# A transformer block on one core: keys and queries stored unsplit and split a group ahead, half of the weight pieces quantised in the first part

## The chip, the cores and the metric

One NeuronCore of a Trainium2 chip runs the whole program. The metric is the device time of one execution in microseconds (us); lower is better. Two changes are told apart only where they differ by more than the spread of repeated runs.

## The reference, cut to what matters

Input x is (8, 1024, 512) fp32. The block is x + attention(layernorm(x)), then x + ffn(layernorm(x)). Attention has 16 heads, a latent of 128 for queries and one for keys and values, 32 plain and 16 rotated dimensions per head, a causal mask and a clip of the scores at +-80. The rotated key part is shared by all heads. The feed-forward part quantises activations and weights to FP4 in blocks of 16.

```python
c_q, c_kv = x @ W_DQ, x @ W_DKV
Qc, Kc, V = heads(c_q @ W_UQ), heads(c_kv @ W_UK), heads(c_kv @ W_UV)
Qr, Kr = rope(heads(c_q @ W_QR)), rope(x @ W_KR)
scores = clip(concat(Qc, Qr) @ concat(Kc, Kr).T, -80, 80)
out = softmax(causal(scores) / sqrt(48)) @ V @ W_O
# feed-forward: every operand goes through
scale = maximum(max(abs(xb)) / 6, 1e-12)          # xb: blocks of 16
q = GRID[searchsorted(MID, abs(xb / scale))] * sign(xb) * scale
```

## The kernel before

Three parts follow each other, with a barrier at each seam. Every large product is made of three passes over operands split into a rounded part (hi) and its rest (lo): hi x hi, hi x lo, lo x hi.

**Projections** (`projections`, lines 119 to 511): 16 blocks of 512 tokens (8 batches, 2 halves), written once and looped. A block is a list of units, `UNITS1` (line 113): C (both latents, 24 matmuls 512 wide), KR (12), X0 and X1 (16 transposes of the normalised rows of the *next* block), K0, K1, Q0, Q1 (6 each), R0, R1 (rotated queries, 6 each) and V0, V1 (6 each): 84 matmuls and 16 transposes. All units go round four two-bank slots of PSUM. TensorE (lines 448 to 511) works through the list; every engine has the list in its own order of code and waits on counters. ScalarE (292 to 336) casts a unit's bank to hi; VectorE (338 to 446) subtracts it to give lo (`c_lo` line 414, `xt_lo` 373, `kq_out` 442), multiplies the rotated parts by the tables (424 to 430), and computes the next block's row statistics (`row_stats`, 343) and normalised rows (`normalise`, 356, in the code right after C). GpSimd (257 to 290) raises the variances to the power -1/2 (266), adds the two rotated products (285) and, after ScalarE's cast (334), subtracts for their lo (288). SyncE (205 to 255) loads x and stores hi and lo of keys and queries (244), of the rotated parts (238, 247), and V (250). `turned` holds the rotated products. C needs the previous block's X units, X needs the normalised rows, K0 needs `c_lo`.

**Attention** (`attention`, 574 to 1004): 32 groups of 4 heads of one batch, in 12 steps each (`STEPS`, 520): query half 0 with 4 key tiles, half 1 with 8; the diagonal steps are 512, 384, 256 and 128 wide. At step k TensorE makes the scores of k + 1 (20 matmuls, 956) and then weighs step k - 1: P V into `ps_o` (971) and the row sums into `ps_d` (985). ScalarE takes the exponentials (772) and copies `ps_o` out (782); three PSUM slots are shared by score pairs, so the scores of step k + 1 wait for the first exponential of step k. VectorE clips (823, 831), adds pairs of steps (841), turns `ps_d` (848), inverts (852), turns back (856) and normalises (863). In its list by step (875 to 930) stand also the eight instructions that quantise one piece of the feed-forward weights (128x528) per group: reduce 884, scale 889, reciprocal 895, ties 899, product 903, then, after ScalarE's multiply (799), mask 917, two rounding steps 921 and 925, product 930. SyncE (667 to 731) loads a group with 15 transfers (4 for keys and queries in hi and lo, 8 for rotated queries, 2 for rotated keys, 1 for V) and a piece, during the group before, and stores pieces and results.

**Feed-forward** (`feed_forward`, from 1027) is not touched by the change. `fp4_scales` (86) and `fp4_round` (97) are the helpers it shares with the change: `fp4_round` is a mask (100) and two rounding steps (102, 104), each behind a wait for the one before (`own`). GpSimd there multiplies by the inverse scales (1209), released by VectorE's line 94.

## Time and profile before

| | us |
|---|---|
| median of 3 runs | 3201.62 (3198.46 to 3202.04) |
| the profiled execution | 3199.42 |
| its span, first to last instruction | 3197.6 |

| busy, of the span | us | share |
|---|---|---|
| TensorE | 3045.5 | 95% |
| TensorE weight loads | 2234.2 | 70% |
| VectorE | 2604.2 | 81% |
| ScalarE | 1221.9 | 38% |
| GpSimd | 668.1 | 21% |

Engines in the rows: PE is TensorE, PEld its weight loads, DVE VectorE, ACT ScalarE, POOL GpSimd, SPq SyncE's queue. A timeline row gives start and length in us, engine, line, instruction, output and inputs, form, how many were merged (xN), and in brackets the idle time before it and what ended it. Matmuls overlap, so their rate is read from starts. A row by line and form ends with busy us, mean ns of one, and the idle time before. In the table by stage each engine has its busy us and its count of instructions; then come the granted clock of TensorE (1.00 is full), the DMA engines' share and GB/s.

### The profile page before, as it was taken

To read this page: it belongs to the slowest core of one execution; us is meant where nothing else is said; L and a number is where in the kernel's file an instruction comes from. 1 tells how busy PE (TensorE), PEld (TensorE's weight loads), DVE (VectorE), ACT (ScalarE), POOL (GpSimd) and SP (SyncE) were. 2 spreads that over 40 slices of the span, in tenths; PEclk is the share of its full clock that TensorE was granted. 3 is DMA by queue.
4 is the path that set the end of the run, shared out by engine and by line. 5 is a ranking of instruction groups with operands and counts; after the bars stand their busy time and mean duration, and the time that the engine had idled before them with its cause. 6 is when DMAs were issued, how large, how long until landed. Compare 5 with 4: busy or idle time off the path is not lost.

```text
span 3197.6 us, 65496 instructions
## 1 busy us (share of the span) xinstructions
PE 3045.5 (95%) x23492; PEld 2234.2 (70%) x23492; DVE 2604.2 (81%) x4427; ACT 1221.9 (38%) x1830; POOL 668.1 (21%) x634
## 2 busy tenths in 40 slices
PE   7999679999999999978999999999999999999999
PEld 6777534444444444446888888888888888888887
DVE  6777457888888888887888888888888888888886
ACT  3444346666666666652222222222222222222221
POOL 2334300000000000012332332232322222223322
PEclk9999889999999999998999999999999999999999
DMA  6999956665656666651000000000000000000000
GB/s 234 334 338 341 314 151 170 161 182 160 184 169 160 179 167 181 172 160 50 30 25 28 30 26 29 30 30 30 30 30 30 30 30 30 30 30 30 30 24 14
DMA packets 234506, 351.37 MB, mean 110 GB/s; under 512 B 17616, under 2 KB 117840, under 8 KB 234448
## 3 DMA queue, kind: packets, MB, share of 16 engines
q1 hardware_dynamic: 234448, 350.59, 35.9%
q8 instruction: 37, 0.61, 0.1%
q14 instruction: 21, 0.17, 0.0%
HBM read 205.55 MB, written 144.97 MB: 110 GB/s over the span
## 4 chain that ended last, share of the span: by engine, by line
PE 54%; DVE 1%; ACT 0%; issue 0%; POOL 0%; DVEq 0%
PE p_ring L1464 30%; PE p_ring L1492 15%; PE p_ring L1444 5%; PE p_ring L1482 2%; PE p_ring L1472 1%; DVE sb_wg_lo L1391 0%; PE p_ring L1504 0%; DVE sb_fp_tmp L102 0%; DVE sb_xq L1351 0%; DVE sb_h_amax L88 0%; DVE sb_stage L1362 0%; DVE sb_ht_lo L1380 0%; DVE sb_xq L1337 0%; DVE sb_stats L1326 0%; DVE sb_xq L104 0%
## 5 line engine op out<-in xcount | busy, mean ns | idle before, releaser
L772 ACT ACTIVATE sb_probs<-scores 128x1024 f32<-128x1024 f32 (+3 forms) x768 | 586.0, 813 | 395.9 <-PE scores L956 384.9
L1464 PE MATMUL p_ring<-sb_wg_hi,sb_xq_hi 128*128 128x512 f32 (+1 forms) x1536 | 458.5, 379 | 0.3 <-DVE sb_wd_lo L1391 0.3
L1464 PE MATMUL p_ring<-sb_wg_lo,sb_xq_hi 128*128 128x512 f32 (+1 forms) x1536 | 448.9, 373 | 0.0
L1464 PE MATMUL p_ring<-sb_wg_hi,sb_xq_lo 128*128 128x512 f32 (+1 forms) x1536 | 447.9, 373 | 0.0
L831 DVE TENSOR_SCALAR sb_probs<-sb_probs 128x2048 f32<-128x2048 f32 (+3 forms) x320 | 288.3, 901 | 91.6 <-ACT sb_probs L772 88.5
L971 PE MATMUL ps_o<-sb_probs,sb_v 128*32 128x512 f32 (+3 forms) x3072 | 328.1, 499 | 0.0
L1209 POOL TENSOR_TENSOR sb_stage<-sb_stage,sb_h_inv 128x512 f32<-128x512 f32 (+1 forms) x192 | 210.6, 1097 | 542.0 <-DVE sb_h_inv L94 542.0
L956 PEld LDWEIGHTS scores<-sb_q_hi,sb_k_hi 32*128 32x128 f32 x1536 | 73.7, 182 | 345.4 <-ACT sb_probs L772 284.4
L1464 PEld LDWEIGHTS p_ring<-sb_wg_hi,sb_xq_lo 128*128 128x128 f32 x1536 | 285.5, 188 | 41.5
L1464 PEld LDWEIGHTS p_ring<-sb_wg_lo,sb_xq_hi 128*128 128x128 f32 x1536 | 285.0, 188 | 41.1
L1464 PEld LDWEIGHTS p_ring<-sb_wg_hi,sb_xq_hi 128*128 128x128 f32 x1536 | 277.0, 189 | 36.3 <-issue 0.7
L1262 ACT ACTIVATE sb_stage<-p_ring 128x512 f32<-128x512 f32 (+1 forms) x192 | 106.7, 556 | 468.3 <-PE p_ring L1464 468.2
L1492 PE MATMUL p_ring<-sb_wd_hi,sb_ht_hi 128*128 128x512 f32 x704 | 280.2, 398 | 2.2 <-DVE sb_ht_lo L1380 2.2
L1492 PE MATMUL p_ring<-sb_wd_hi,sb_ht_lo 128*128 128x512 f32 x704 | 274.5, 390 | 0.0
L1492 PE MATMUL p_ring<-sb_wd_lo,sb_ht_hi 128*128 128x512 f32 x704 | 274.1, 389 | 0.0
L823 DVE SCALAR_TENSOR_TENSOR sb_probs<-sb_probs,sb_bound 128x512 f32<-128x512 f32 x256 | 174.6, 682 | 121.9 <-ACT sb_probs L772 121.9
L956 PE MATMUL scores<-sb_q_hi,sb_k_hi 32*128 32x512 f32 (+3 forms) x1536 | 172.6, 439 | 89.3 <-DMA sb_v<-v 40.1
L1215 POOL TENSOR_TENSOR sb_stage<-sb_stage,sb_h_scale 128x512 f32<-128x512 f32 (+1 forms) x192 | 189.7, 988 | 267.8 <-DVE sb_stage L104 267.8
L1275 ACT CAST sb_ht_hi<-p_ring 128x1024 fp32r<-128x1024 f32 (+1 forms) x128 | 95.1, 744 | 384.0 <-PE p_ring L1482 384.0
L743 POOL TENSOR_TENSOR sb_wo_lo<-sb_x,sb_wo_hi 128x2048 fp32r<-128x2048 f32 x1 | 9.3, 9316 | 1008.0 <-ACT sb_wo_hi L802 1008.0
L102 DVE SCALAR_TENSOR_TENSOR sb_fp_tmp<-sb_stage 128x512 f32<-128x512 f32 (+1 forms) x192 | 206.0, 1073 | 6.6
L1253 ACT ACTIVATE sb_stage<-sb_stage 128x512 f32<-128x512 f32 (+1 forms) x192 | 113.9, 593 | 215.5 <-POOL sb_stage L1209 215.5
(141 smaller groups left out, 5957.4 us busy)
## 6 DMA issues: line engine op xcount, KB each, us to landing
kq<-sb_kq_out SPq DMA_DIRECT2D x64, 1024.0 KB, 8.6
sb_xin<-in_L_attn_x_dram SPq DMA_DIRECT2D x32, 512.0 KB, 5.9
...
```

What stands on the lines that cost most here:

```text
L102: dve.scalar_tensor_tensor(out=tmp, in0=big, scalar=1.5, in1=y, op0=ALU.max, op1=ALU.add).then_inc(sem, 1)
L772: act.activation(probs[:, k % PROBS, 2 * pair:2 * pair + 2, off:BANK], scores[(2 * k + pair) % RING2][:, :, off:BANK], ACT.Exp, scale=SCAL ...
L823: i = dve.scalar_tensor_tensor(out=pr, in0=pr, scalar=P_MIN, in1=bound[:].unsqueeze(1).to_broadcast([P, NI, P]), op0=ALU.max, op1=ALU.min)
L831: i = dve.tensor_scalar(pr, pr, P_MAX, P_MIN, ALU.min, ALU.max)
L956: mm = pe.matmul(scores[(2 * k + i // 2) % RING2][:, i % 2, off:BANK], key[s][rows, keys], query[s][rows, queries], start=(n == 0), stop=( ...
L971: mm = pe.matmul(ps_o[rows, off:BANK], v_sb[s][:, j, rows], probs[:, k % PROBS, i, off:BANK], start=(j == 0), stop=last)
L1209: pool.tensor_tensor(x, x, spread(h_inv[:, a // QB:b // QB], (b - a) // QB), ALU.mult).then_inc(h_y, 1)
L1215: pool.tensor_tensor(x, x, spread(h_scale[:, a // QB:b // QB], (b - a) // QB), ALU.mult).then_inc(h_q, 1)
L1253: act.mul(h_big[:, h_slot(r, s), 0:b - a], h[:, a:b], MAGIC).then_inc(h_magic, 1)
L1444: i = pe.matmul(ps[:, 0, :], at[a][:, g, :], wo[b][:, g, :], start=(g == 0 and a == b == 0), stop=(g == GROUPS - 1 and a == 1))
L1464: i = pe.matmul(ps[:, m, 0:b0 - a0], xt[a][:, c, :], wg[b][:, m, c, a0:b0], start=(c == 0 and a == b == 0), stop=(c == DC - 1 and a == 1))
L1492: i = pe.matmul(ps[:, 0, :], ht[a][:, c, :], wd[b][:, c, :], start=(c == 0 and a == b == 0), stop=(c == FC - 1 and a == 1))
```

## The change

**First part.** Keys and queries are stored once, unsplit: ScalarE copies the bank to fp32 and frees it, and VectorE's subtraction is gone. C becomes C0 (keys' and values' latent) and C1 (queries'), each with its own cast and rest. The even and odd halves of the rotated pairs are now kept in separate planes, so one unit R (6 matmuls) gives both; VectorE multiplies each of its two banks by two table planes at once (two instructions, 1024 wide), and GpSimd's addition and subtraction and ScalarE's cast for R are 1024 wide. The banks are freed through two counters. One weight piece per block is quantised: `fp4_scales` and a product after X1, ScalarE's multiply after Q1, `fp4_round` and a product after R; SyncE loads and stores it behind the block's stores. The rope table has four planes in place of two, the weights one 256-column stretch less.

**Attention.** A group's keys and queries come with two transfers into `kq_raw`, issued two bodies ahead when the buffer's last split is done. ScalarE rounds them at steps 1 and 2 of the group before, VectorE takes the rest at steps 3 and 9, and TensorE waits for both at step 0. The 16 pieces left take two groups each: scales in the even one, rounding in the odd. Half 0 is turned at step 4 (before: 3), inverted and turned back at step 10 (4, 5), normalised at step 11 (6), ahead of the turning of half 1. Pieces are stored from step 4 of odd groups; in the last body W_O and the third part's first loads are issued behind that store.

```diff
-UNITS1 = ["C", "KR", "X0", "X1", "K0", "K1", "Q0", "Q1", "R0", "R1", "V0", "V1"]
+UNITS1 = ["C0", "C1", "KR", "X0", "X1", "K0", "K1", "Q0", "Q1", "R", "V0", "V1"]
 UNITS1_LAST = [u for u in UNITS1 if u[0] != "X"]
-HI1 = ["C", "X0", "X1", "K0", "K1", "Q0", "Q1", "V0", "V1"]
+HI1 = ["C0", "C1", "X0", "X1"]
+FREED_BY_ACT = ["K0", "K1", "Q0", "Q1", "V0", "V1"]
+FREED_BY_DVE = ["C0", "C1", "KR", "X0", "X1", "R"]
...
-            sp.dma_start(cos_sin[:], t["rope"].rearrange("k p t -> p k t")).then_inc(s_rope, 16)
+            sp.dma_start(qr_raw[:], t["W_QR"]).then_inc(s_w, 16)
+            sp.dma_start(rope[:], t["rope"].rearrange("k p t -> p k t")).then_inc(s_rope, 16)
             sp.wait_ge(xin_free, 2)
             load_x(0, 1)
+            sp.dma_start(piece_in[:], t["w_all"][0]).then_inc(piece_loaded, 16)
...
-                    for s in range(2):
-                        sp.dma_start(kq_v[k, s, b, :, :, cols], kq_out[:, half, k, s]).then_inc(stored[half], 16)
-                sp.wait_ge(rope_lo, n * 3 + 3 + 3)
+                    freed(sp, n, name)
+                    sp.dma_start(kq_v[k, b, :, :, cols], kq_out[:, half, k]).then_inc(stored[half], 16)
+                sp.wait_ge(rope_lo, n * 2 + 2 + 2)
                 for s in range(2):
-                    sp.dma_start(rq_v[s, b, :, :, cols], r_out[:, half, s]).then_inc(stored[half], 16)
-                sp.wait_ge(ps_free, unit(n, units.index("V1")) + RING1 + 1)
+                    for c in range(2):
+                        sp.dma_start(rq_v[s, c, b, :, :, cols], r_out[:, half, s, c]).then_inc(stored[half], 16)
+                freed(sp, n, "V1")
                 for j in range(4):
                     sp.dma_start(v_v[b, half * 4 + j],
                                  v_out[:, half, j].rearrange("p (g d) -> p g d", g=GROUPS)).then_inc(stored[half], 16)
+                if not last:
+
+                    sp.wait_ge(piece_ready, n + 1)
+                    sp.dma_start(piece_in[:], t["w_all"][n + 1]).then_inc(piece_loaded, 16)
+                sp.wait_ge(piece_done, n + 1)
+                sp.dma_start(t["wq_all"][n], piece_y[:]).then_inc(piece_stored, 16)
...
+                for k, name in enumerate(("KR", "R")):
                     if name == "KR":
-                        tu = turned[0:DR, k]
-                        lo = kr_out[0:DR, half, 1, :]
-                        hi = kr_out[0:DR, half, 0, :]
+                        a, b_ = turned_kr[:, 0, :], turned_kr[:, 1, :]
+                        hi, lo = kr_out[0:DR, half, 0, :], kr_out[0:DR, half, 1, :]
                     else:
-                        tu = turned[:, k]
-                        lo = r_out[:, half, 1, k - 1, :]
-                        hi = r_out[:, half, 0, k - 1, :]
-
-                    pool.wait_ge(ps_free, unit(n, units.index(name)) + RING1 + 1)
-                    pool.tensor_tensor(tu[:, 0, :], tu[:, 0, :], tu[:, 1, :], ALU.add).then_inc(rope_sum, 1)
-
-                    pool.wait_ge(rope_hi, n * 3 + k + 1)
-                    pool.tensor_tensor(lo, tu[:, 0, :], hi, ALU.subtract).then_inc(rope_lo, 1)
+                        a, b_ = turned[:, 0], turned[:, 1]
+                        hi, lo = r_out[:, half, 0], r_out[:, half, 1]
+
+                    (freed_last if last else freed)(pool, n, name)
+                    pool.tensor_tensor(a, a, b_, ALU.add).then_inc(rope_sum, 1)
+
+                    pool.wait_ge(rope_hi, n * 2 + k + 1)
+                    pool.tensor_tensor(lo, a, hi, ALU.subtract).then_inc(rope_lo, 1)
...
-                        act.copy(kq_out[:, half, k, 0, 2 * m:2 * m + 2, :].bitcast(F32R), ps[:]).then_inc(act_hi, 1)
+                        act.copy(kq_out[:, half, k, 2 * m:2 * m + 2, :], ps[:]).then_inc(act_free, 1)
...
+                    if name == "K1":
+                        act.wait_ge(rope_sum, n * 2 + 1)
+                        act.copy(kr_out[0:DR, half, 0, :].bitcast(F32R), turned_kr[:, 0, :]).then_inc(rope_hi, 1)
+                    if name == "Q1":
+                        act.wait_ge(piece_ready, n + 1)
+                        act.mul(piece_big[:], piece_y[:], MAGIC).then_inc(piece_magic, 1)
+                    if name == "V1":
+                        act.wait_ge(rope_sum, n * 2 + 2)
+                        act.copy(r_out[:, half, 0].bitcast(F32R), turned[:, 0]).then_inc(rope_hi, 1)
...
-                dve.wait_ge(stored[half], b * STORES1 + STORES1)
...
+                        dve.tensor_tensor(c_lo[:, k], ps[:, 0], c_hi[:, k].bitcast(F32),
+                                          ALU.subtract).then_inc(dve_free, 1)
+                        if k == 1 and not last:
                             normalise(n + 1)
...
+                    elif name == "R":
+                        pos = slice(half * BANK, (half + 1) * BANK)
+                        dve.wait_ge(ps_ready, number + 1)
+
+                        dve.wait_ge(rope_lo, n * 2 + 2)
+                        dve.tensor_tensor(turned[:, 0], ps[:, 0, :].unsqueeze(1).to_broadcast([P, 2, BANK]),
+                                          rope[:, 1:3, pos], ALU.mult)
+                        dve.tensor_tensor(turned[:, 1], ps[:, 1, :].unsqueeze(1).to_broadcast([P, 2, BANK]),
+                                          rope[:, 0:2, pos], ALU.mult).then_inc(dve_free, 1)
...
-                    else:
-                        k, m = "KQ".index(name[0]), int(name[1])
-                        dve.wait_ge(act_hi, hi_count)
-                        pair = slice(2 * m, 2 * m + 2)
-                        dve.tensor_tensor(kq_out[:, half, k, 1, pair, :], ps[:], kq_out[:, half, k, 0, pair, :],
-                                          ALU.subtract).then_inc(ps_free, 1)
+                        rest_of_x(int(name[1]), slot(units, name), hi_count,
+                                  (n + 1) * len(FREED_BY_DVE) + (FREED_BY_DVE.index("X1") + 1))
+                    if name == ("KR" if last else "X1"):
+
+                        dve.wait_ge(piece_loaded, n * 16 + 16)
+                        fp4_scales(dve, piece_in[:], piece_amax[:], piece_scale[:], piece_inv[:], piece_scaled,
+                                   n * SCALES_STEPS)
+                        own(dve, piece_scaled, n * SCALES_STEPS + SCALES_STEPS)
+                        dve.wait_ge(piece_stored, n * 16 + 16)
+                        dve.tensor_tensor(blocks_of(piece_y[:]), blocks_of(piece_in[:]), spread(piece_inv[:], WP // QB),
+                                          ALU.mult).then_inc(piece_ready, 1)
+                    if name == "R":
+                        y = blocks_of(piece_y[:])
+                        dve.wait_ge(piece_magic, n + 1)
+                        fp4_round(dve, piece_y[:], piece_big[:], piece_tmp[:], piece_rounded, n * ROUND_STEPS)
+                        own(dve, piece_rounded, n * ROUND_STEPS + ROUND_STEPS)
+                        dve.tensor_tensor(y, y, spread(piece_scale[:], WP // QB), ALU.mult).then_inc(piece_done, 1)
...
+            def load_raw(it2, s):
+
+                g = it2 * 2 + s
+                sp.wait_ge(raw_split, g * 2 + 2)
+                for k in range(2):
+                    sp.dma_start(kq_raw[:, k], t["kq"][k, bass.ds(g * NI, NI)].rearrange("i p t -> (i p) t")
+                                 ).then_inc(raw_loaded, 16)
...
-                get(k_hi[s][:], t["kq"][0, 0, heads].rearrange("i p t -> (i p) t"))
-                get(q_hi[s][:], t["kq"][1, 0, heads].rearrange("i p t -> (i p) t"))
-                get(k_lo[s][:], t["kq"][0, 1, heads].rearrange("i p t -> (i p) t"))
-                get(q_lo[s][:], t["kq"][1, 1, heads].rearrange("i p t -> (i p) t"))
...
+            load_raw(0, 0)
             load(0, 0)
+            load_piece(0)
+            load_raw(0, 1)
             load(0, 1)
 
             def body(it2, s, first, last):
                 if not first:
-                    before = (it2, 0) if s == 1 else (it2 - 1, 1)
-                    store_piece(*before)
                     if not last:
 
                         sp.wait_ge(pv_done, step_no(it2, s, 0) + PROBS)
                         load(*following(it2, s))
-                    store(*before, 1)
+                    store(*preceding(it2, s), 1)
+                if s == 0:
+                    if not (isinstance(it2, int) and it2 == G2 - 1):
+
+                        sp.wait_ge(w_y, it2 + 1)
+                        load_piece(it2 + 1)
+                else:
+                    store_piece(it2)
+                if not (isinstance(it2, int) and it2 == G2 - 1):
+                    load_raw(it2 + 1, s)
...
+            def round_raw(it2, s, k):
+
+                act.wait_ge(raw_loaded, it2 * 64 + (s * 32 + 32))
+                act.copy((k_hi, q_hi)[k][s][:], kq_raw[:, k]).then_inc(raw_rounded, 1)
...
-                    if k == 6:
-                        act.wait_ge(w_y, it2 * 2 + (s + 1))
-                        act.mul(w_big[:], w_sb[:, s, :], MAGIC).then_inc(w_magic, 1)
+                    if k in (1, 2) and not last:
+                        round_raw(*following(it2, s), k - 1)
+                    if k == 6 and s == 0:
+                        act.wait_ge(w_y, it2 + 1)
+                        act.mul(w_big[:], w_sb[:], MAGIC).then_inc(w_magic, 1)
...
+            def rest_of_raw(it2, s, k):
+
+                dve.wait_ge(raw_rounded, it2 * 4 + (s * 2 + k + 1))
+                dve.tensor_tensor((k_lo, q_lo)[k][s][:], kq_raw[:, k], (k_hi, q_hi)[k][s][:].bitcast(F32),
+                                  ALU.subtract).then_inc(raw_split, 1)
...
                     elif k == 3:
+                        if not last:
+                            rest_of_raw(*following(it2, s), 0)
+                        if s == 0:
+                            own(dve, w_scaled, scaled + 3)
+                            dve.tensor_scalar(w_inv[:], w_inv[:], TIES, None, ALU.mult).then_inc(w_scaled, 1)
+                    elif k == 4:
                         turn(it2, s, 0)
-                        own(dve, w_scaled, scaled + 3)
-                        dve.tensor_scalar(w_inv[:], w_inv[:], TIES, None, ALU.mult).then_inc(w_scaled, 1)
-                    elif k == 4:
-                        invert(it2, s, 0)
-                        own(dve, w_scaled, scaled + 4)
-                        dve.tensor_tensor(w, w, spread(w_inv[:], WP // QB), ALU.mult).then_inc(w_y, 1)
+                        if s == 0:
+                            own(dve, w_scaled, scaled + 4)
+                            dve.wait_ge(w_stored, it2 * 16 + 16)
+                            dve.tensor_tensor(w, blocks_of(w_in[:]), spread(w_inv[:], WP // QB),
+                                              ALU.mult).then_inc(w_y, 1)
+                        else:
+                            own(dve, w_rounded, rounded + 3)
+                            dve.tensor_tensor(w, w, spread(w_scale[:], WP // QB), ALU.mult).then_inc(w_done, 1)
                     elif k == 5:
-                        turn_back(it2, s, 0)
                         add_up(it2, s, 0, 0)
                     elif k == 6:
-                        normalise(it2, s, 0)
                         add_up(it2, s, 0, 1)
                     elif k == 7:
-                        if len(SUMS) > 1:
-                            add_up(it2, s, 1, 0)
+                        add_up(it2, s, 1, 0)
                     elif k == 8:
-                        if len(SUMS) > 1:
-                            add_up(it2, s, 1, 1)
-                        dve.wait_ge(w_magic, piece + 1)
-                        dve.tensor_scalar(w_bits, w_bits, EXPONENT, TOP_MANTISSA, ALU.bitwise_and,
-                                          ALU.bitwise_or).then_inc(w_rounded, 1)
+                        add_up(it2, s, 1, 1)
                     elif k == 9:
-                        own(dve, w_rounded, rounded + 1)
-                        dve.scalar_tensor_tensor(out=w_tmp[:], in0=w_big[:], scalar=1.5, in1=w_all, op0=ALU.max,
-                                                 op1=ALU.add).then_inc(w_rounded, 1)
+                        if not last:
+                            rest_of_raw(*following(it2, s), 1)
                     elif k == 10:
-                        own(dve, w_rounded, rounded + 2)
-                        dve.scalar_tensor_tensor(out=w_all, in0=w_big[:], scalar=1.5, in1=w_tmp[:], op0=ALU.max,
-                                                 op1=ALU.subtract, reverse1=True).then_inc(w_rounded, 1)
+                        invert(it2, s, 0)
+                        turn_back(it2, s, 0)
                     elif k == 11:
+                        normalise(it2, s, 0)
                         turn(it2, s, 1)
...
+                    pe.wait_ge(raw_split, it2 * 4 + (s * 2 + 2 + 2))
```

## Rows read from the trace of the kernel before

**Rows 1.** Busy time by stage: stretch, length, PE, PEld, DVE, ACT, POOL, clock, DMA, GB/s
```profile
42.00:375.40 333.40, 325.59 (x1500) 261.75 (x1499) 250.88 (x408) 157.67 (x208) 131.19 (x106) 1.00 0.97 333
375.40:414.30 38.90, 0.00 (x0) 0.00 (x0) 0.00 (x0) 2.27 (x3) 4.20 (x6) 0.56 0.92 279
414.30:1405.10 990.80, 940.49 (x13312) 450.30 (x13312) 816.81 (x1243) 627.91 (x865) 5.36 (x1) 0.99 0.61 168
```

**Rows 2.** Timeline of TensorE, one block of the first part (start, length)
```profile
200.50 0.40 PE L468 MATMUL p_ring<-sb_xt_hi,sb_w_hi 128*128 128x512 f32 x1
...
208.65 0.40 PE L468 MATMUL p_ring<-sb_xt_hi,sb_w_lo 128*128 128x512 f32 x1
209.60 2.00 PE L458 MATMUL p_ring<-sb_ident,sb_xhat 128*128 128x128 f32 x16 [0.55 <-DVE sb_xhat L362]
...
222.63 0.40 PE L468 MATMUL p_ring<-sb_xt_hi,sb_w_hi 128*128 128x512 f32 x1
```

**Rows 3.** Timeline of VectorE, the same block
```profile
203.11 2.47 DVE L348 BATCH_NORM_STATS2 sb_stats<-sb_xin 128x6 f32<-128x512 f32 x4 [3.35 <-DVEq L437]
...
206.15 0.17 DVE L354 TENSOR_SCALAR sb_vareps<-sb_moments 128x4 f32<-128x4 f32 x1
207.33 1.22 DVE L414 TENSOR_TENSOR sb_c_lo<-p_ring,sb_c_hi 128x1024 fp32r<-128x1024 f32 x1 [1.01 <-ACT sb_c_hi L318]
208.47 1.91 DVE L362 TENSOR_SCALAR sb_xhat<-sb_xin,sb_moments,sb_rstd 128x512 f32<-128x512 f32 x4
...
220.02 0.68 DVE L429 TENSOR_TENSOR sb_turned<-p_ring,sb_cos_sin 128x512 f32<-128x512 f32 x1
```

**Rows 4.** Timeline of ScalarE, the same block
```profile
206.29 1.01 ACT L318 CAST sb_c_hi<-p_ring 128x1024 fp32r<-128x1024 f32 x1 [2.42 <-PE p_ring L468]
...
222.10 0.62 ACT L334 CAST sb_r_out<-sb_turned 128x512 fp32r<-128x512 f32 x1 [3.86 <-POOL sb_turned L285]
```

**Rows 5.** Timeline of GpSimd, the same block
```profile
206.40 1.01 POOL L266 TENSOR_TENSOR sb_rstd<-sb_vareps,sb_mhalf 128x4 f32<-128x4 f32 x1 [1.16 <-DVE sb_vareps L354]
...
220.78 1.30 POOL L285 TENSOR_TENSOR sb_turned<-sb_turned 128x512 f32<-128x512 f32 x1 [3.46 <-DVE sb_turned L429]
```

**Rows 6.** Timeline of VectorE in the third part, around 2009 us
```profile
2009.35 0.43 DVE L100 TENSOR_SCALAR sb_x_big<-sb_x_big 128x512 int32<-128x512 int32 x1
2009.81 1.43 DVE L102 SCALAR_TENSOR_TENSOR sb_fp_tmp<-sb_x_big,sb_xq 128x512 f32<-128x512 f32 x1
2011.27 0.69 DVE L104 SCALAR_TENSOR_TENSOR sb_xq<-sb_x_big,sb_fp_tmp 128x512 f32<-128x512 f32 x1
```

**Rows 7.** Timeline of GpSimd in the third part, around 2009 us
```profile
2009.51 1.19 POOL L1209 TENSOR_TENSOR sb_stage<-sb_stage,sb_h_inv 128x512 f32<-128x512 f32 x1 [6.77 <-DVE sb_h_inv L94]
```

**Rows 8.** Groups by line and form: VectorE (from 1560 us), GpSimd, ScalarE (to 380 us)
```profile
L102 DVE SCALAR_TENSOR_TENSOR sb_fp_tmp<-sb_x_big,sb_xq 128x512 f32<-128x512 f32 x59 | 84.5, 1432 | 2.0
...
L1209 POOL TENSOR_TENSOR sb_stage<-sb_stage,sb_h_inv 128x512 f32<-128x512 f32 x128 | 149.7, 1169 | 493.6 <-DVE sb_h_inv L94 493.6
L1209 POOL TENSOR_TENSOR sb_stage<-sb_stage,sb_h_inv 128x384 f32<-128x384 f32 x64 | 60.9, 952 | 48.5 <-DVE sb_h_inv L94 48.5
...
L295 ACT CAST sb_w_hi<-sb_v_out 128x3584 fp32r<-128x3584 f32 x1 | 3.2, 3177 | 9.9 <-DVE sb_v_out L394 9.9
```

**Rows 9.** Timelines of VectorE, TensorE and ScalarE at a group's first steps
```profile
824.15 0.71 DVE L848 STREAM_TRANSPOSE sb_d_turned<-ps_d 128x512 f32<-128x512 f32 x1
...
825.51 1.04 PE L985 MATMUL ps_d<-sb_probs,sb_ones 128*32 128x512 f32 x8
...
827.29 0.66 ACT L772 ACTIVATE sb_probs<-scores 128x256 f32<-128x256 f32 x2 [1.34 <-PE scores L956]
```

**Rows 10.** Busy time of two us at a group's end (columns as rows 1)
```profile
820.00:822.00 2.00, 1.91 (x32) 0.87 (x29) 0.35 (x1) 1.30 (x2) 0.00 (x0) 1.00 0.00 0
```

**Rows 11.** Timeline of SyncE's DMA issues, the first of attention
```profile
391.13 0.36 SPq L671 DMA_DIRECT2D sb_k_hi<-kq  x1
```

**Rows 12.** DMA issues of the page (KB each, median us to landing)
```profile
kq<-sb_kq_out SPq DMA_DIRECT2D x64, 1024.0 KB, 8.6
```

229 lines of the change are left out of this document (123 added, 106 removed).

## The prediction

> **What bounds the kernel now.** I read the stages first, then one block of the first part engine by engine, then one group of the second part.
>
> The table by stage [rows 1] shows the first part with TensorE and the DMA engines both near full (325.59 us of 333.40; share 0.97), then 38.90 us without a matmul, then attention with TensorE 95% busy. The third part keeps its code and is costed at nothing.
>
> In a block of the first part [rows 2] matmuls start every (208.65 - 200.50) / 35 = 0.233 us, at full clock. C and KR, 36 of them, last 8.40 us, so TensorE could turn x at 208.90; it waits until 209.60 for the normalised rows. From there to the next C are 13.03 us: 48 matmuls (11.20) and 1.83 for the 16 transposes and the changeovers. A block takes 222.63 - 200.50 = 22.13 us.
>
> VectorE in that block [rows 3]: row statistics take 3.21 us (203.11 to 206.32), a 1024-wide subtraction 1.22 (1.14 before the next starts), and the first half of the normalisation is through 1.00 us after its start, with TensorE 0.13 later. GpSimd's power takes 1.01 and starts 0.08 after the variances; its 512-wide addition takes 1.30 and starts 0.08 after the product it waits for [rows 3, 5]; I cost its subtraction alike. ScalarE's 512-wide cast starts 0.02 after GpSimd's addition; a bank is seen 0.42 after its last matmul starts (200.50 + 23 x 0.233 to 206.29) [rows 4].
>
> In attention a step is TensorE work in some places and the loop score, exponential, next score in the others. ScalarE idles 1.34 us before the 256-wide exponentials of step 3 [rows 9].
>
> **The change in the first part.** It takes away R1: 6 matmuls of 84, 1.40 us a block, and with C split in two and no subtractions for keys and queries the normalised rows should come in time. TensorE alone would need 8.40 + 1.83 + 42 x 0.233 = 20.03 us a block. DMA goes from 4 MB of keys and queries a block to 2, plus 0.5 MB of pieces: no bound any more.
>
> But VectorE gets a chain between R and the next block's statistics: the rounding of a weight piece, four instructions, three of them with both inputs in SBUF. The same signal that starts it starts GpSimd's addition for R, which also reads two SBUF operands and is now 1024 wide. What that does the third part shows [rows 6, 7]: VectorE frees GpSimd and goes on to the exponent mask (0.43 us); GpSimd starts at 2009.51; the next VectorE instruction starts at 2009.81 and ends only at 2011.24, 0.54 after GpSimd's end at 2010.70. It takes 1432 ns as a mean of 59, all alike [rows 8], where the following one of the same kind takes 0.69. So one engine waits for the other for a whole instruction. The first part of before has no such pair at a tight place, so this wait is new.
>
> GpSimd at 1024 wide isn't in the trace. From 384 to 512 columns it grows by 217 ns [rows 8], which gives 1.30 + 4 x 0.217 = 2.16 us; twice the 512-wide one gives 2.60. I take 2.38, the middle, as neither end is nearer. The Trainium skill's page "GPSIMD Engine Reference", under side-by-side cycle accounting, has 4497 ns for 2048 columns; halved, an estimate, that is 2.25 us, and by it the sum would be 14 x 0.26 = 3.6 us less.
>
> Now the block, in us from the start of C0. R is ready at -2.61 (last matmul at -3.03). The two 1024-wide products end at -0.25. GpSimd starts at -0.17, waits 0.11 for the mask, ends at 2.33. The first rounding step then ends at 2.87, the second runs from 2.90 to 3.61, and the last product could start at 3.64. Meanwhile ScalarE's cast, 0.62 at 512 columns and 3.18 at 3584 [rows 4, 8], so 1.05 at 1024, runs from 2.35 to 3.40, and GpSimd asks for its subtraction at 3.48, 0.16 ahead of VectorE. I take it that it gets in, as in [rows 6, 7], where it asked while a VectorE instruction ran and got in before the next. It ends at 5.86, the product at 6.40. Statistics to 9.54, power to 10.63, the rests of C0 and C1 beside it to 10.75, first normalised half 11.70, transposes at 11.83. TensorE was ready at 8.40. Period 11.83 + 1.83 + 9.80 = 23.46, 1.33 longer than now. The extremes of GpSimd's width give 0.44 less or more.
>
> The piece's scales (two 528-wide instructions like the 0.69 of [rows 6] and three small ones, about 2.3 us) lie while TensorE does K and Q (5.6 us), where the subtractions stood; some 2 us stay as cover for a late piece load. ScalarE's multiply lies in its idle time there.
>
> Sum for the part: 14 blocks at +1.33 = +18.6; the first block, with no rounding before it, -2.1 (1.40 and its stall of 0.70); the last, with no X, -1.4; the preparation, 256 columns fewer on ScalarE and then on VectorE at 0.9 to 1.1 ns each, -0.5. The larger rope load lies under the preparation: 0. Together **+14.6**, from +8 to +21.
>
> **The seam.** From the last matmul (375.4) it is 15.7 us to the first load of attention [rows 1, 11] and 23.2 more to the first score. Afterwards R's rest ends 5.9 after the last matmul; nine store issues at 0.4 us [rows 11] and 3.7 of landing, an estimate, make 13.2, as little is queued by then: -2.5. The first group loads 3 MB, not 4: at the 279 GB/s of [rows 1] 3.8 us less, and some 0.7 since the second group doesn't press behind it. The splits run under the remaining loads. **-7**, from -1 (only R's later store shows) to -12.
>
> **Attention.** Two casts on ScalarE (1.05 each) go into the 1.34 us before the exponentials of step 3 [rows 9] and the longer idle time before those of step 4: 0. VectorE gets two subtractions (1.14 each) and loses half of a piece, whose five wide instructions at 0.6, mask and three small ones are some 3.9: 0, because the half-0 normalisation has left the steps with the sums, and step 9's product waits for TensorE, not the other way. The raw load is issued at about 819, when the DMA engines fall idle [rows 10]; 1 MB at 279 GB/s is 3.8 us, and ScalarE asks at 827.29 - 1.34 = 825.95: 0. One thing moves the wrong way: the half-0 normalisation (0.60) now stands ahead of the transpose that frees ps_d. It ended at 824.86, and would at 825.47, where TensorE's first ps_d matmul is at 825.51 and must load weights first [rows 9]: 0.12 a group, 31 times, **+3.7**, from 0 to +6. In the last group W_O is loaded later, about 1 us on ScalarE, against a product less at the end: 0, +-2.
>
> **Sum**: +14.6 - 7 + 3.7 = +11.3 on the profiled execution's 3199.4 us. Its time lies 2.2 under the median of the runs shown, 3201.6; the same difference on the median gives 3213. This case's own range is 3200 to 3225.
>
> **Rivals.** *A, the product gets in before the subtraction.* The lead is 0.16 us out of six summed terms; a cast of 1.24 (twice 0.62) turns it round. Then the product ends at 4.34, the transposes start at 9.77, period 21.40: 14 x -0.73 - 4.0 = -14.2, in all -17.5: **3184**. *N, TensorE sets the pace.* If the engines don't get in each other's way, the transposes wait at most 0.1 and the block is 20.03: 14 x -2.10 - 4.0 = -33.4, in all **3165**. For it speaks TensorE's and the DMAs' load in rows 1; against it the 59 equal waits. [...] *M, the two orders take turns* or A's gain is lost at a late piece load: within 6 us of now, **3201**. *R, the raw load is late too*: if it lands 8.6 us after issue, as the key stores do [rows 12], ScalarE's cast ends near 828.7 and holds back steps 3 and 4 by some 0.45 us; 30 groups, +13 on the forecast: **3226**. It decides from a landing over 7 us; the idle DMA engines speak against it.
>
> **How the numbers follow.** Forecast 0.46, A 0.22, N 0.12, M 0.12, R 0.08. Of the forecast a fifth lies within 0.2% (6.4 us, about what a measurement of this kernel can tell from no change). Slower 0.37 + 0.08 = 0.45; same 0.09 + 0.12 = 0.21; faster 0.34. The range leaves out N and the tails: 3176 (A less 8) to 3228.
>
> **What would show it.** In the profile after: the first rounding step of the piece (128x528) at some 2.7 us where the second takes 0.70, and the last product at 2.9 (forecast) or 0.69 (A). Transposes that wait for the normalised rows over 3 us a block (A 1.4, N none). The stretch without a matmul down from 38.9 to about 32. Attention up by some 4 us from 990.8. Rounding steps of 0.70 all through, or statistics that start under 2.5 us after C0, prove me wrong.

## The result, and the profile after the change

The changed kernel takes **3360.3 us** (median of 4 runs, 3357.5 to 3361.9) against 3200.9 for the kernel before in the same comparison: a ratio of **1.0499, 95% interval 1.0485 to 1.0513**. It is slower by 5%, far above the range of the forecast. Its profiled execution has a span of 3360.2 us, 162.6 more than before.

From TensorE's timeline (start of the first C0, of the first part's last matmul, of the first score, of the last row of matmuls into ps_d), in us:

| kernel | first part | seam | attention | rest |
|---|---|---|---|---|
| before | 353.1 | 39.5 | 990.3 | 1792.9 |
| after | 399.1 | 43.3 | 1106.7 | 1789.7 |
| difference | +46.0 | +3.8 | +116.4 | -3.2 |

The page of the changed kernel, granted clock in 40 slices and the queue that fetches instructions (packets, MB, share), then that queue in the kernel before:

```profile
PEclk8898969999999999998899999999999999999999
q8 instruction: 154, 2.52, 0.3%
...
q8 instruction: 37, 0.61, 0.1%
```

Busy time by stretch of the changed kernel (columns as rows 1); the first three answer to [rows 1]:

```profile
42.00:420.90 378.90, 332.17 (x1405) 271.86 (x1403) 306.32 (x463) 166.79 (x220) 128.83 (x74) 0.91 0.71 230
420.90:463.90 43.00, 0.06 (x5) 0.05 (x4) 11.75 (x9) 5.49 (x6) 5.36 (x5) 0.53 0.80 194
463.90:1570.90 1107.00, 981.37 (x13312) 468.83 (x13312) 838.93 (x1162) 679.52 (x911) 7.15 (x2) 0.94 0.44 115
...
158.40:162.50 4.10, 4.06 (x18) 3.97 (x19) 3.12 (x6) 1.43 (x3) 1.26 (x1) 0.50 0.97 296
...
738.00:748.00 10.00, 7.29 (x72) 3.98 (x72) 2.87 (x6) 4.09 (x6) 0.00 (x0) 0.52 0.18 56
```

Two things are new: the granted clock is 0.91 in the first part where it was 1.00, and the same 13312 matmuls of attention take 116 us longer.

Timeline of TensorE after the change, a block of the first part (it answers to [rows 2]) and a turn of attention's loop:

```profile
146.54 0.40 PE L508 MATMUL p_ring<-sb_xt_hi,sb_w_hi 128*128 128x512 f32 x1
...
154.71 0.40 PE L508 MATMUL p_ring<-sb_xt_hi,sb_w_lo 128*128 128x512 f32 x1
158.44 3.67 PE L498 MATMUL p_ring<-sb_ident,sb_xhat 128*128 128x128 f32 x16 [3.33 <-DVE sb_xhat L398]
...
172.65 0.40 PE L508 MATMUL p_ring<-sb_xt_hi,sb_w_hi 128*128 128x512 f32 x1
...
734.03 0.61 PE L1075 MATMUL ps_d<-sb_probs,sb_ones 128*32 128x256 f32 x8
738.29 0.69 PE L1046 MATMUL scores<-sb_q_hi,sb_k_hi 32*128 32x384 f32 x4 [3.64 <-issue]
...
742.03 0.69 PE L1046 MATMUL scores<-sb_q_lo,sb_k_hi 32*128 32x384 f32 x2 [2.42 <-issue]
```

In the block TensorE waits 3.33 us for the normalised rows (0.55 before), and the transposes and the first matmuls behind them run at a clock of 0.50, the 1.2 GHz level. In the loop it waits twice, right behind the return to the loop's top, for nothing that the profile shows, 6.06 us together, and then runs at the lower clock as well (0.52 from 738 to 748 us, above).

VectorE after the change, the same block [rows 3], and the last block:

```profile
145.18 1.22 DVE L465 TENSOR_TENSOR sb_turned<-p_ring,sb_rope 128x1024 f32<-128x1024 f32 x1
146.31 0.43 DVE L100 TENSOR_SCALAR sb_piece_big<-sb_piece_big 128x528 int32<-128x528 int32 x1
146.77 2.79 DVE L102 SCALAR_TENSOR_TENSOR sb_piece_tmp<-sb_piece_big,sb_piece_y 128x528 f32<-128x528 f32 x1
149.59 0.71 DVE L104 SCALAR_TENSOR_TENSOR sb_piece_y<-sb_piece_big,sb_piece_tmp 128x528 f32<-128x528 f32 x1
150.34 2.79 DVE L484 TENSOR_TENSOR sb_piece_y<-sb_piece_y,sb_piece_scale 128x528 f32<-128x528 f32 x1
153.05 2.46 DVE L384 BATCH_NORM_STATS2 sb_stats<-sb_xin 128x6 f32<-128x512 f32 x4
...
419.14 0.70 DVE L88 TENSOR_REDUCE sb_piece_amax<-sb_piece_in 128x33 f32<-128x528 f32 x1 [6.59 <-DMA sb_piece_in<-in_ffn_weights_dram]
...
421.46 1.22 DVE L463 TENSOR_TENSOR sb_turned<-p_ring,sb_rope 128x1024 f32<-128x1024 f32 x1
```

GpSimd in the same block [rows 5]:

```profile
146.47 2.53 POOL L316 TENSOR_TENSOR sb_turned<-sb_turned 128x1024 f32<-128x1024 f32 x1 [3.45 <-DVE sb_turned L465]
150.16 2.40 POOL L319 TENSOR_TENSOR sb_r_out<-sb_turned,sb_r_out 128x1024 f32<-128x1024 f32 x1 [1.16 <-ACT sb_r_out L369]
```

This is the mechanism of the forecast: L102 starts 0.30 us behind GpSimd's addition and ends 0.56 behind its end, L484 starts 0.18 behind the subtraction and ends 0.57 behind it, while L104, which meets neither, takes 0.71.

SyncE's DMA issues at the seam, after the change [rows 11]:

```profile
415.05 0.87 SPq L282 DMA_DIRECT2D sb_piece_in<-in_ffn_weights_dram  x1
...
429.89 2.48 SPq L274 DMA_DIRECT2D rq<-sb_r_out  x4
...
441.12 0.84 SPq L724 DMA_DIRECT2D sb_kq_raw<-kq  x2
```

### The profile page after: what moved, and what is told of

The parts are those of the page before. It is cut to its first block, busy times and chain, and to the rows that moved or that the text cites. A ratio compares the mean times of both kernels' runs of the same rounds, so it can differ in the third digit from the quotient of the medians.

```text
span 3360.2 us, 64924 instructions
## 1 busy us (share of the span) xinstructions
PE 3094.3 (92%) x23396; PEld 2264.0 (67%) x23396; DVE 2688.3 (80%) x4411; ACT 1286.8 (38%) x1894; POOL 663.1 (20%) x602
## 3 DMA queue, kind: packets, MB, share of 16 engines
q8 instruction: 154, 2.52, 0.3%
## 4 chain that ended last, share of the span: by engine, by line
PE 52%; DVE 1%; ACT 0%; issue 0%; POOL 0%; DVEq 0%
PE p_ring L1554 29%; PE p_ring L1582 14%; PE p_ring L1534 5%; PE p_ring L1572 2%; PE p_ring L1562 1%; PE p_ring L1594 0%; DVE sb_wg_lo L1481 0%; DVE sb_fp_tmp L102 0%; DVE sb_xq L1441 0%; DVE sb_h_amax L88 0%; DVE sb_stage L1452 0%; DVE sb_ht_lo L1470 0%; ACT sb_wg_hi L1369 0%; DVE sb_xq L1427 0%; DVE sb_stats L1416 0%
## 5 line engine op out<-in xcount | busy, mean ns | idle before, releaser
L1061 PE MATMUL ps_o<-sb_probs,sb_v 128*32 128x512 f32 (+3 forms) x3072 | 338.3, 514 | 3.7 <-DVE sb_probs L899 3.7
L102 DVE SCALAR_TENSOR_TENSOR sb_fp_tmp<-sb_stage 128x512 f32<-128x512 f32 (+1 forms) x192 | 205.9, 1072 | 6.6
```

The costliest lines, as they stand in the source:

```text
L102: dve.scalar_tensor_tensor(out=tmp, in0=big, scalar=1.5, in1=y, op0=ALU.max, op1=ALU.add).then_inc(sem, 1)
L1061: mm = pe.matmul(ps_o[rows, off:BANK], v_sb[s][:, j, rows], probs[:, k % PROBS, i, off:BANK], start=(j == 0), stop=last)
```

## The experiments

### Attention: the place of the loop among the fetched instructions

The profile shows 117 more instruction packets, and a packet is 2.52 MB / 154 = 16.4 KB. The loop runs 14 turns, so 13 times back to its top: 117 = 13 x 9. TensorE's part of one turn is 832 matmuls and 832 weight loads (13312 / 16) and 39 waits, register and branch instructions, 1703, in the kernel before, and 1705 after, with the new wait for the split keys. The first part's program became shorter, so the loop begins at TensorE's instruction 2481 where it began at 2535 (the instructions recorded in the traces give the same distance, 54, and the same lengths). In the trace of the kernel before no instruction packet falls between 541 and 1345 us, that is from the end of the loop's first turn to the end of its last; in the changed kernel's they come all through the loop. Four kernels take these apart.

**a_pad54** and **a_pad179**, the changed kernel, and **b_pad202**, the kernel before, get instructions that wait for nothing (two waits make one instruction):

```
             pe.wait_ge(s_id, 16)
+            for _ in range(108):        # 358 in a_pad179, 404 in b_pad202
+                pe.wait_ge(s_id, 16)
```

> The changed kernel with 54 instructions that wait for nothing added to TensorE's program at the start of the first part, so that the attention loop (1705 instructions with this one's waits, 1703 before) begins at instruction 2535 of TensorE's program as in the kernel before, and not at 2481. Theory P (place): attention lost 115 us because each turn of the loop has its instructions fetched again, and whether it does depends on where the loop lies against the borders of the fetched blocks. Then the two idle stretches put down to issue at the loop's turn (3.9 and 2.9 us) go, a turn takes 61.4 to 61.8 us where it takes 69.8, instruction packets fall from 154 to about 37, time 3360 - 115 = about 3245 us. Theory L (length): the two instructions that the loop gained are what no longer fits: 3360, 154 packets. Theory W (the new wait for the split keys, or their late load, is what costs): 3360 as well.

> The kernel before with 202 such instructions at the start, which puts its attention loop at instruction 2737: 256 more than 2481, where the changed kernel has it, and nothing else. P: the kernel before now loses what the change lost in attention, 3201 + 115 = about 3316 us, with about 150 instruction packets and a turn of about 69 us. L and W: 3201, 37 packets, 61.4 us a turn.

**b_loop_wait**, the kernel before with the loop's two more instructions:

```
                     pe.wait_ge(loaded[s], it2 * LOADS2 + LOADS2)
+                    pe.wait_ge(loaded[s], it2 * LOADS2 + LOADS2)
```

> The kernel before with the wait for the group's loads written twice, which gives its attention loop the two more instructions (1705) that the change gives it, at the same place but for one instruction. L: about 3316 us and 150 instruction packets. P and W: 3201 and 37.

> a_pad54 with 125 more instructions of padding: the attention loop begins at instruction 2660. Theory P with the sizes of the Trainium skill's page 'Runtime: NRT & Kernel Launch', Instruction fetch mechanics (blocks of 256 instructions; TensorE holds 2048, so eight): a loop of 1705 instructions touches seven blocks if it begins in the first 87 places of one, and eight otherwise; the good start (2535, that is 231 past a multiple of 256) and this one (100 past) can't both lie within 87, so attention loses its 89 to 111 us again: 3340 to 3365 in all, some 154 instruction packets. If only some few places are bad (a border inside one critical spot of the loop), this one is as good as 2535: 3250.

| kernel | loop begins at | past a multiple of 256 | packets | attention | time, ratio to before |
|---|---|---|---|---|---|
| before | 2535 | 231 | 37 | 990.3 | 3200.2 |
| b_loop_wait | 2536 | 232 | 37 | 989.9 | 3201.2, 1.0001 [0.9992, 1.0011] |
| a_pad54 | 2535 | 231 | 37 | 995.3 | 3249.9, 1.0153 [1.0136, 1.0170] |
| after | 2481 | 177 | 154 | 1106.7 | 3360.3, 1.0499 [1.0485, 1.0513] |
| b_pad202 | 2737 | 177 | 155 | 1079.0 | 3303.4, 1.0318 [1.0301, 1.0336] |
| a_pad179 | 2660 | 100 | 154 | 1068.9 | 3332.4, 1.0408 [1.0391, 1.0425] |

From the page of b_pad202, then attention by the table of stretches, then its timeline of TensorE at the loop's turn:

```profile
q8 instruction: 155, 2.54, 0.3%
```

```profile
428.20:1507.60 1079.40, 972.39 (x13312) 466.61 (x13312) 820.24 (x1243) 630.14 (x865) 5.34 (x1) 0.95 0.56 156
```

```profile
766.32 0.45 PE L958 MATMUL scores<-sb_q_hi,sb_k_hi 32*128 32x384 f32 x4 [2.56 <-issue]
...
769.10 0.69 PE L958 MATMUL scores<-sb_q_lo,sb_k_hi 32*128 32x384 f32 x2 [1.99 <-issue]
```

The kernel before, with none of the change, gets two waits at the same matmuls, lower clock behind them and 88.7 us more in attention (and 13 us at its start, where C0 now begins at 34.7 instead of 21.8: the padding's own price). The changed kernel, moved by 54 instructions, has neither wait. Theory P holds, L and W fall: the length (b_loop_wait) and the new wait (in a_pad54 it is still there) cost nothing. Attention's loss by fetching is 1106.7 - 995.3 = **111.4 us**, 8.6 for each return to the top: 6.0 of waits on the mean of the 13 returns, the rest at the lower clock.

b_pad202 loses less than the 115 expected, and a_pad179 with 73.6 us less than its 89 to 111 (C0 begins at 31.6 in it, 10 us of padding). What a return costs is not the same in the three: the waits are 6.0, 4.8 and 3.9 us on the mean of 13 returns in the changed kernel, b_pad202 and a_pad179, and the granted clock is at its lower level around them for 112, 88 and 75 us in all. Why they differ, the first two with the loop at the same place past a multiple of 256, no run shows.

The rule that a_pad179's expectation works out (a loop that touches seven blocks stays, one that touches eight is fetched anew) can be fitted to every kernel in the table, but only with the blocks' borders shifted. If they lay at the multiples of 256 of this count, the two good starts would touch eight blocks too (231 + 1703 is more than 7 x 256 = 1792). It fits if a border lies 178 to 231 past each multiple, and nothing here shows where it lies. What is shown is that the place decides; the number of blocks is argued. The Trainium skill's page "Runtime: NRT & Kernel Launch", section Instruction fetch mechanics, gives blocks of 16 KiB and 256 instructions and 2048 instructions for TensorE, and the packets agree with the block. Its sentence "The IRAM is only 2 cache lines" doesn't fit: a loop of 1703 instructions, more than six such blocks, ran 14 times without being fetched again. That the eighth place is kept for the block to come is an inference, and where the good places end was not tried.

### The first part: two engines, then a queue

**a_no_round** leaves the rounding of the first part's pieces out (on a_pad54's basis, as all that follow except a_round_early):

```
-   fp4_round(dve, piece_y[:], piece_big[:], piece_tmp[:], piece_rounded, n * ROUND_STEPS)
-   own(dve, piece_rounded, n * ROUND_STEPS + ROUND_STEPS)
-   dve.tensor_tensor(y, y, spread(piece_scale[:], WP // QB), ALU.mult).then_inc(piece_done, 1)
+   dve.sem_inc(piece_done, 1)
```

> a_pad54 without the four rounding instructions of the first part (the pieces quantised there are stored scaled but not rounded: that part of the result is left out), everything else where the change has it. Theory S (these four, behind R and beside GpSimd's additions, are the first part's loss): block 20.0 to 20.3 us, first part about 320 us, seam down by 3 to 5 us, 3165 to 3175. If the loss comes from the rest of the change there (1024-wide additions, C in two banks, later power, the scales): 3230 or more.

3182.6 us, 0.9942 [0.9926, 0.9959], above the 3165 to 3175 expected: first part 331.2 us where a_pad54 has 397.4, and a seam that didn't shrink (43.8 against 42.1). The four instructions were 66 of the 77 us that a_pad54 lies above case N (353.1 - 33.4 = 319.7). Of the rest, part is a late load of the piece (VectorE waits 3 to 4 us for it in each block), part the same meeting of engines with other instructions. VectorE and GpSimd of a_no_round, by their timelines:

```profile
174.03 2.13 DVE L390 TENSOR_SCALAR sb_vareps<-sb_moments 128x4 f32<-128x4 f32 x1
```

```profile
173.74 2.39 POOL L319 TENSOR_TENSOR sb_r_out<-sb_turned,sb_r_out 128x1024 f32<-128x1024 f32 x1 [1.16 <-ACT sb_r_out L369]
```

An instruction on four columns, 0.17 us elsewhere [rows 3], takes 2.13: here one input from SBUF was enough.

**a_round_early** keeps the rounding and puts it ahead of R's products:

```
-                    if name == "Q1":          # ScalarE: piece_big = piece_y * MAGIC
+                    if name == "Q0":
...
-                    if name == "R":           # VectorE: fp4_round and the last product
+                    if name == "Q1":
```

> The changed kernel with the rounding of a weight piece (four VectorE instructions) in front of R's products and not behind them, and ScalarE's multiply for it after Q0 and not after Q1: VectorE then rounds while GpSimd has no wide operation. Theory S (the first part lost its time to VectorE and GpSimd waiting for each other, and to TensorE's lower granted clock behind each stall): the first rounding step and the last product take 0.7 us instead of 2.79, the transposes wait under 0.5 us instead of 3.3, the 16 transposes take 2.0 instead of 3.6, a block takes 20.0 to 20.6 us instead of 25.1: 15 x -4.7 = -70, and R's rest and so the seam some 3 to 5 us less: about 3286. Rival D (the blocks are long because of the stores or of a clock that falls anyway): the block stays over 24 us, 3345 to 3360. Rival C (the rounding now holds back R's products, the next statistics come late and GpSimd's power waits for its addition): half of the gain, about 3320. Attention keeps its 69.8 us a turn in each.

3347.6 us, a gain of 13 where theory S said 74. VectorE and GpSimd of a_round_early, by their timelines:

```profile
135.56 0.71 DVE L88 TENSOR_REDUCE sb_piece_amax<-sb_piece_in 128x33 f32<-128x528 f32 x1 [3.79 <-DMA sb_piece_in<-in_ffn_weights_dram]
...
139.03 0.71 DVE L102 SCALAR_TENSOR_TENSOR sb_piece_tmp<-sb_piece_big,sb_piece_y 128x528 f32<-128x528 f32 x1
...
140.52 0.71 DVE L484 TENSOR_TENSOR sb_piece_y<-sb_piece_y,sb_piece_scale 128x528 f32<-128x528 f32 x1
```

```profile
147.13 2.40 POOL L319 TENSOR_TENSOR sb_r_out<-sb_turned,sb_r_out 128x1024 f32<-128x1024 f32 x1 [1.16 <-ACT sb_r_out L369]
149.50 1.02 POOL L300 TENSOR_TENSOR sb_rstd<-sb_vareps,sb_mhalf 128x4 f32<-128x4 f32 x1
```

The meeting is gone as expected (0.71 twice), and two waits stand in its place. The piece's load comes late (VectorE waits 2.5 to 3.8 us for it in the blocks, 3.79 in this one), because SyncE issues it behind the stores of R and V, and the power starts at 149.50 behind the subtraction, though its input was ready at 146.61. The power behind GpSimd's work is rival C's mechanism. The time lies in rival D's range, and most blocks take some 24 us, as D had it; a_early_load below rules D out, as moving that one load makes the first part 19 us shorter than here, where D allowed 5. The first part is 21.6 us shorter, not 70, and the seam 4.6 longer.

Four kernels then take these waits away in turn. **a_early_load** issues the load behind the stores of keys and queries; **a_early_load_pool** also has GpSimd subtract after the next power; **a_store** is a_early_load with the piece's store moved up too; **a_store_add** is a_store with VectorE adding for R (edits abridged, each mark names the kernels that have it):

```
     sp.dma_start(kq_v[k, b, :, :, cols], kq_out[:, half, k]) ...
+    if not last:                                           # from a_early_load on; stood last
+        sp.wait_ge(piece_ready, n + 1)
+        sp.dma_start(piece_in[:], t["w_all"][n + 1]).then_inc(piece_loaded, 16)
+    sp.wait_ge(piece_done, n + 1)                          # from a_store on; stood last
+    sp.dma_start(t["wq_all"][n], piece_y[:]).then_inc(piece_stored, 16)
...
     inverse_deviation(n + 1)                               # a_early_load_pool: GpSimd subtracts
+    rest(n - 1, 1 - half, 1)                               # here for the R of the block before
...
+    dve.tensor_tensor(turned[:, 0], turned[:, 0], turned[:, 1], ALU.add)   # a_store_add
-    pool.tensor_tensor(a, a, b_, ALU.add)                  # a_store_add, for R alone
```

> a_pad54 with the rounding of a_round_early, and with SyncE issuing the load of the next weight piece right behind the stores of keys and queries instead of behind those of R and V. In a_round_early the two engines no longer waited for each other (0.71 us where the changed kernel has 2.79), but the scales waited 2.6 to 3.8 us for that load, and GpSimd's power for the row statistics started 2.9 us late behind R's subtraction (2.40 us). Theory Q (late load and late power are what is left of the first part's loss): with the load in time VectorE is some 3 us earlier, the power still stands behind the subtraction: the transposes wait about 1.3 us, a block 21.4 to 22.0, the first part about 50 us shorter than in a_pad54 (397 us from the first C0 to the last matmul), 3195 to 3205 in all. Rival D (stores and clock set the block): no more than 5 us gained over a_round_early with the same place of the loop, that is about 3235.

> a_early_load, and GpSimd subtracts for the rest of R one power later (the power of the next block's statistics stands ahead of it). Q: the transposes wait under 0.2 us, TensorE sets the pace with 20.0 to 20.3 us a block, first part 320 to 325 us, granted clock 1.00 in it, about 3165 to 3175 in all: faster than the kernel before (3200) by 1%. Rival D: as a_early_load.

> a_early_load with the store of a rounded piece issued right behind the next piece's load, ahead of the stores of R and V. In a_early_load_pool VectorE's product for the piece waited 2.9 us each block for the store of the piece before (39.5 us in 14 blocks), which SyncE had issued last of all; that made R's products late and TensorE wait 0.93 us for their bank and 1.44 for the normalised rows. Theory Q: with that wait gone VectorE is 2 to 3 us earlier; left is GpSimd's order (addition, subtraction, power), which starts the power some 3 us after the statistics: the transposes wait 0.5 to 1.5 us, a block 20.6 to 21.6 us, first part 325 to 345 us (358 in a_early_load), 3180 to 3197 in all. Rival: the wait moves to the load of the rows of x, which SyncE issues behind the stores of R and V: 3200 to 3210.

> a_store with the 1024-wide addition for R on VectorE (1.2 us more for it) instead of GpSimd (2.4 us, and whatever VectorE instruction falls on it waits). Q: R's rest is done 1 us earlier and the power starts at the statistics' end or 1 us behind it, the transposes wait under 0.5 us, a block 20.0 to 20.7, first part 320 to 332 us, 3168 to 3182. Rival: VectorE, now with 19 us of work in a block of 20, is late itself: R's products hold back TensorE's second bank of C, 3190 to 3200.

| kernel | first part | seam | time | ratio to before |
|---|---|---|---|---|
| a_early_load | 358.1 | 45.5 | 3211.6 | 1.0037 [1.0023, 1.0052] |
| a_early_load_pool | 361.2 | 45.5 | 3216.8 | 1.0048 [1.0032, 1.0065] |
| a_store | 349.6 | 39.6 | 3197.9 | 0.9992 [0.9983, 1.0001] |
| a_store_add | 332.0 | 37.1 | 3177.6 | 0.9928 [0.9914, 0.9941] |

a_early_load came out 7 us above its expected range: the store of the last piece, issued last of all, now holds back the next product (16.8 us in all from 60 to 370 us). a_early_load_pool, meant to reach 3170, was no faster than it. Its VectorE, grouped by line and form from 60 to 370 us:

```profile
L487 DVE TENSOR_TENSOR sb_piece_y<-sb_piece_in,sb_piece_inv 128x528 f32<-128x528 f32 x14 | 9.9, 708 | 39.5 <-DMA wq_all<-sb_piece_y 39.5
```

Its timelines, VectorE and then GpSimd:

```profile
143.53 1.58 DVE L408 TENSOR_SCALAR sb_xhat<-sb_xin,sb_moments,sb_rstd 128x512 f32<-128x512 f32 x1
```

```profile
141.45 1.01 POOL L300 TENSOR_TENSOR sb_rstd<-sb_vareps,sb_mhalf 128x4 f32<-128x4 f32 x1 [0.72 <-DVE sb_vareps L400]
142.44 2.39 POOL L310 TENSOR_TENSOR sb_r_out<-sb_turned,sb_r_out 128x1024 f32<-128x1024 f32 x1
```

39.5 us of waiting for a store, and the normalisation's first instruction (0.54 us elsewhere) now meets the subtraction that was moved: 1.58. With the store moved (a_store) the kernel stands level with before, and with one 2.4 us GpSimd instruction fewer (a_store_add) it is **0.7% faster than the kernel before**. The timeline of TensorE of a_store_add, the transposes of one block and then a whole other one:

```profile
52.37 2.01 PE L503 MATMUL p_ring<-sb_ident,sb_xhat 128*128 128x128 f32 x16 [0.77 <-DVE sb_xhat L399]
...
147.86 0.40 PE L513 MATMUL p_ring<-sb_xt_hi,sb_w_hi 128*128 128x512 f32 x1
...
156.34 2.01 PE L503 MATMUL p_ring<-sb_ident,sb_xhat 128*128 128x128 f32 x16
...
167.97 0.40 PE L513 MATMUL p_ring<-sb_xt_hi,sb_w_hi 128*128 128x512 f32 x1
```

The block from 147.86 has no wait in front of its transposes and takes 167.97 - 147.86 = 20.11 us, case N's 20.03. It is the only one of 15 that does: the others take 20.95 to 21.38, most with the 0.77 us of waiting for the normalised rows that the first line shows, and the part is still 12 us above case N.

### Attention's other 5 us

At a good place attention takes 995.3 us, 5.0 above before. **a_turn_first** and **a_wo_split** change a_store_add (995.0) at one place each:

```
-    normalise(it2, s, 0)          # a_turn_first
     turn(it2, s, 1)
+    normalise(it2, s, 0)
...
-    pool.tensor_tensor(ahead.wo_lo[:], ahead.x1[:], ahead.wo_hi[:].bitcast(F32), ALU.subtract)
+    for c in range(GROUPS):       # a_wo_split
+        i = pool.tensor_tensor(ahead.wo_lo[:, c], ahead.x1[:, c], ahead.wo_hi[:, c].bitcast(F32), ALU.subtract)
```

> a_store_add with two VectorE instructions of attention changed round at a group's end: the transpose that frees ps_d before the normalisation of the first half. With the loop at a good place attention takes 995.0 to 995.3 us in every variant of the changed kernel and 990.3 before. Theory T (the prediction's: the normalisation ahead of the transpose delays TensorE's next ps_d matmuls): 3 to 5 us less in attention, about 991, and 3173 to 3175 in all. Rival: the 5 us come from the casts or subtractions of the raw keys and queries in steps 2 to 4 or from the later group load: attention stays at 995, 3178 in all.

> a_store_add with GpSimd's subtraction for the rest of W_O (128x2048, one instruction in attention's last group) in four instructions of 128x512. In a_pad54 that instruction runs from 1448.00 to 1452.55; VectorE's clip of the last but one step (128x512, 0.68 us elsewhere) starts at 1448.93 and ends at 1453.09, and TensorE waits 3.02 us for it. In the kernel before the same two met the other way round: GpSimd's took 9.32 us and VectorE's none longer. Theory E (attention's 5 us over before are this meeting): the clip takes 0.7 to 1.9 us, TensorE's wait of 3.0 falls to 0.5 to 1.8, attention 992 to 994 (995.0), some 1.5 to 3 us less in all than a_store_add's 3177.6. Rival (it is the late W_O load or the casts that hold the last steps): attention stays at 995.

a_turn_first: attention 993.9, 1.1 us less and not the 3 to 5 of theory T, which falls. Even the 1.1 can't be put down to the order: 0.7 of them lie in attention's first 150 us, where the traces of a_pad54 and a_store_add, which have the same order, are over 1 us apart. The total, 3180.2, 0.9934 [0.9921, 0.9948], can't be told from a_store_add's. The 5 us come all at the end: up to the last but one step a_pad54's attention is level with the one before (983.7 us from the first score in both). a_wo_split: attention 992.9, as theory E said; the total, 3177.4, 0.9926 [0.9913, 0.9940], doesn't show it against a_store_add's 3177.6. The meeting, in a_pad54's timelines of GpSimd, VectorE and TensorE:

```profile
1448.00 4.55 POOL L804 TENSOR_TENSOR sb_wo_lo<-sb_x,sb_wo_hi 128x2048 fp32r<-128x2048 f32 x1 [1008.49 <-ACT sb_wo_hi L872]
```

```profile
1448.93 4.16 DVE L893 SCALAR_TENSOR_TENSOR sb_probs<-sb_probs,sb_bound 128x512 f32<-128x512 f32 x1 [0.85 <-ACT sb_probs L838]
```

```profile
1454.55 1.08 PE L1063 MATMUL ps_o<-sb_probs,sb_v 128*32 128x256 f32 x8 [3.02 <-DVE sb_probs L901]
```

and in a_wo_split's of VectorE and TensorE:

```profile
1379.55 0.90 DVE L897 SCALAR_TENSOR_TENSOR sb_probs<-sb_probs,sb_bound 128x512 f32<-128x512 f32 x1 [1.14 <-ACT sb_probs L842]
```

```profile
1383.61 0.43 PE L1067 MATMUL ps_o<-sb_probs,sb_v 128*32 128x128 f32 x8 [0.61 <-DVE sb_probs L897]
```

The clip falls from 4.16 to 0.90. The matmul that waited 3.02 us no longer waits; the 0.61 stands in front of the next one into ps_o. So theory E is right for some 2 of the 5 us, by one trace of each kernel. The rest remains, as the four short instructions meet the next clips (1.50 and 1.77 us) and TensorE waits 0.95 us for an exponential just before. In the kernel before, VectorE had no gap at that place, GpSimd waited for it (9.32 us for the same instruction), and TensorE lost nothing; VectorE waited only behind its last clip, off the path.

## Why the prediction was wrong, point by point

- **The block up to the transposes: right.** R's products, the first rounding step (2.7 forecast, 2.79 measured), the subtraction that gets in ahead of the last product (by 0.16 us; 0.18), that product (2.9; 2.79), transposes after C0 (11.83; 158.44 - 146.54 = 11.90). Case A did not happen. GpSimd's addition, taken at 2.38 us, took 2.53, and the subtraction 2.40. The prediction's other estimate, 2.25, halved from the figure for 2048 columns on the Trainium skill's page "GPSIMD Engine Reference", section Elementwise — side-by-side cycle accounting, is a little low against both.
- **The step "Period 11.83 + 1.83 + 9.80 = 23.46": mis-sized.** From the transposes to the next C0 it took 172.65 - 158.44 = 14.21 us, not 11.63. The step priced matmuls behind a 3.4 us wait at the full clock of [rows 2], where the longest wait was 0.55. The clock was granted at 0.50 behind it (the stretch from 158.40 above), and periods of 25.1 and 26.1 us alternate, as the granted clock stays low for longer in one block than in the next. TensorE has no other wait of over 0.3 us in these blocks. The part was 46 us longer, not 14.6. This alone would have put the time out of the range (3213 + 31 = 3244), and a_pad54, the changed kernel without the fetching, takes 3249.9.
- **The seam, "-7, from -1 to -12": wrong in sign, +3.8.** R's rest was taken to end 5.9 us after the last matmul, as in any block. In the last block the scales come two transposes earlier and the piece's load, which the last block alone has no cover for, is late: VectorE idles 6.59 us in front of L88 and starts R's products at 421.46, 0.9 us after the last matmul (420.6). R's stores are issued 9.3 us after it and attention's first load 20.5, against 391.13 - 374.9 = 16.2 before [rows 11]. Two more terms of the step were off. The nine stores were priced at 0.4 us each and took 429.89 to 437.06, 0.8 each; the 3.7 of landing, for which no row was given, came out at 4.1. And from the first load to the first score it took 22.8 us, where 23.2 - 4.5 = 18.7 was forecast: the 279 GB/s used for it are the mean of the whole seam, stores included (334 GB/s up to the first load before, 242 behind it), and the loads now ran at 190 with the DMA engines 0.97 busy. I had counted "some 2 us as cover" for a block with transposes and not looked at the one without.
- **Attention, "+3.7": the step that decided the miss.** It costed what each engine executes and not where its program lies. 111.4 us come from the fetching of TensorE's loop, which no row of before could show, as there it fetched nothing between its first turn and its last; what could be seen was that the program ahead of the loop changes. The normalisation ahead of the transpose, priced 0.12 a group, is worth at most 0.04 and can't be told from nothing. a_pad54's +5.0 belongs to the step "W_O is loaded later ... 0, +-2": TensorE waits 0.67 us for an exponential that stands behind ScalarE's later cast, VectorE has a gap of 0.85 us in front of the clip, and in it GpSimd's subtraction got in first.
- **The casts and subtractions of raw keys and queries, and the raw load: right at nothing.** Between the first score and the last but one step a_pad54 takes 983.7 us, before 983.7. Case R did not happen: the load lands in 4.3 us on the page.
- **The sign** came out as forecast, and would have without the fetching (a_pad54 is 49.7 us slower than before); but 111 of the 159 us have nothing to do with the mechanism that the forecast rests on.
- **The sum** for what was foreseen (a block with a full-clock period, attention without fetching) missed 46 - 14.6 = 31 us in the first part, 11 in the seam and 113 in attention, against 3 gained in the rest.
